# A graph layer's kernel: five edge groups gather normalised rows instead of weighted ones, and the weighted rows are made in the edge steps

## What is computed

```python
N_NODES, D, E = 6250, 512, 100000        # dst is sorted and dense at low numbers
xn = layernorm(x)
gnn = segment_sum(edge_weight[:, None] * xn[src], dst) @ Wg + bg
q, k = elu(xn @ Wq + bq) + 1, elu(xn @ Wk + bk) + 1   # 8 heads of 64
v = xn @ Wv + bv
mix = (q * z) @ (k^T v) @ Wp + bp        # linear attention, z = 1 / (q . sum of k)
x = x + gnn + mix
z = layernorm(x)
# FFN of 512 -> 256 -> 512 whose weights are merged by a gate: mean over rows of
# relu(z @ gfc1^T) @ gfc2^T gives 8 factors; W1m = W1 + sum g_e tv_W1[e], likewise b1, W2, b2
h = relu(z @ W1m^T + b1m)
out = x + layernorm(z + h @ W2m^T + b2m) * lng + lnb
```

## Time and profile before

| | us |
|---|---|
| median of 3 timed executions | 1598.65 (1595.19 to 1599.21) |
| the profiled execution | 1604.54, span 1602.7 |
| PE busy | 1385.1 (86%) |
| DVE busy | 1015.7 (63%) |
| POOL busy | 843.4 (53%) |
| ACT busy | 648.3 (40%) |
| mean granted clock of PE | 0.946 |
| moved by DMA | 366.46 MB |

### The profile page before, as it was taken

The page is one execution under the profiler, slowest core; times in us unless marked ns, Lnnn a source line. Parts: engine busy times, 40 slices in busy tenths (PEclk is TensorE's granted clock), DMA queues, the critical chain, the costliest instruction groups (busy, mean ns, idle before and its releaser), DMA issues. The chain is left out here.

```text
span 1602.7 us, 24972 instructions
## 1 busy us (share of the span) xinstructions
PE 1385.1 (86%) x7963; PEld 605.9 (38%) x7963; DVE 1015.7 (63%) x2041; ACT 648.3 (40%) x1045; POOL 843.4 (53%) x882
## 2 busy tenths in 40 slices
PE   4988978898889888998898988998995998889893
PEld 2544423333333333333333433433342443633331
DVE  7978634344343434385666667877878675448997
ACT  4787722222222322033333323333333665256663
POOL 0001267777777777477777777777771000033432
PEclk9999989999999999699999999999997999899996
DMA  6989678888888888477777777777777879514432
GB/s 214 312 310 341 242 247 274 272 267 271 261 260 274 268 267 290 138 238 237 230 237 236 237 229 234 240 242 250 230 224 183 220 197 223 158 60 151 157 138 85
DMA packets 201553, 366.46 MB, mean 229 GB/s; under 512 B 77101, under 2 KB 82879, under 8 KB 201441
## 3 DMA queue, kind: packets, MB, share of 16 engines
q0 software_dynamic: 62720, 205.57, 41.9%
q1 hardware_dynamic: 138000, 158.43, 30.7%
q10 hardware_dynamic: 720, 1.06, 0.2%
HBM read 287.93 MB, written 65.38 MB: 220 GB/s over the span
## 5 line engine op out<-in xcount | busy, mean ns | idle before, releaser
L1165 POOL DMA_INDIRECT rows<-y_rows,idxT x516 | 492.4, 954 | 184.6 <-issue 165.7
L919 ACT ACTIVATE mb<-bank,ones,ncols 128x512 f32<-128x512 f32 x98 | 76.3, 779 | 445.8 <-PE bank L1964 445.8
L1519 DVE SCALAR_TENSOR_TENSOR acc<-bank,maskt,acc 128x512 f32 x196 | 138.0, 746 | 102.3 <-PE bank L2072 81.9
L2060 PE MATMUL bank<-rows,hots 128*32 128x512 f16 x1548 | 118.1, 412 | 55.5 <-DMA rows<-y_rows,idxT 47.2
L1964 PE MATMUL bank<-Wg,xtb 128*128 128x512 f16 x588 | 139.1, 388 | 16.1 <-DVE xtb L1453 8.9
L1964 PE MATMUL bank<-ztg,G 128*128 128x512 f16 (+1 forms) x624 | 130.7, 371 | 15.5 <-DMA ztg<-zhigh 14.1
L1964 PE MATMUL bank<-KVP,qT 128*128 128x512 f16 x588 | 143.9, 397 | 0.0
L1964 PE MATMUL bank<-Wk,xta 128*128 128x512 f16 x588 | 139.5, 388 | 0.0
L1964 PE MATMUL bank<-Wq,xta 128*128 128x512 f16 x588 | 139.2, 388 | 0.0
L1200 POOL TENSOR_TENSOR acc<-acc,lnbb 128x512 f32 (+1 forms) x49 | 66.0, 1349 | 116.4 <-ACT zq L1051 116.4
L2044 PE MATMUL bank<-xr,kh 128*128 128x512 f16 x392 | 123.7, 399 | 2.4 <-DVE kl L1546 2.4
(11 more groups left out here) (311 smaller groups left out, 2428.9 us busy)
## 6 DMA issues: line engine op xcount, KB each, us to landing
xta<-xt_rows SPq DMA_DIRECT2D x98, 256.0 KB
x_rows<-xhl SPq DMA_DIRECT2D x49, 256.0 KB, 3.8
xt_rows<-xtb SPq DMA_DIRECT2D x49, 256.0 KB, 3.9
y_rows<-yb SPq DMA_DIRECT2D x49, 256.0 KB, 3.6
xr<-x_rows SPq DMA_DIRECT2D x49, 256.0 KB
zt_rows<-ztg SPq DMA_DIRECT2D x49, 256.0 KB, 2.3
acc<-in_x SPq DMA_DIRECT2D x48, 256.0 KB, 4.2
xd<-zt_rows SPq DMA_DIRECT2D x12, 1024.0 KB, 5.4
```

Source lines behind the costliest of these rows:

```text
L919: nc.scalar.activation(mb[:, :], of[:, :], ACT.Relu, scale=ncols[:, col:col + 1], bias=ones[:, 0:1]).then_inc(f_min, 1)
L1165: pool.indirect_dma_start(out=row_slot(s, k).rearrange("p a d -> p (a d)"), out_offset=None, in_=y_rows, in_offset=bass.IndirectOffsetOnAx ...
L1519: nc.vector.scalar_tensor_tensor(out=flat(acc, tile + m), in0=edge_bank(n)[:, :], scalar=maskt[:, m, n:n + 1], in1=flat(acc, tile + m), op ...
L2060: ins = nc.tensor.matmul(edge_bank(n)[W * k:W * k + W, :], hots[:, r, p, :, hot_column(s, k)], row_slot(s, k)[:, q, :], start=s == FIRST[n ...
```

## The change

- The y product, its two evictions and the store of `y_rows` leave the head. They come into the edge steps as slots of their own, -5 to 35 (`y_slots`: six tiles in five slots), from `xta`, which SP loads back from `xt_rows`; the products use four banks.
- The first five groups (16, 8, 8, 8 and 4 steps: XSTEPS = 44 steps) gather from `x_rows`, so POOL's gathers begin when `x_rows` and `xt_rows` are stored. Their placed sums come out transposed (four f32 matmuls of 128 columns), ACT and DVE split them in two f16 halves (`agg_higher`, `agg_lower`), and PE multiplies them by the gnn weight (`weigh`, 12 matmuls); the addition comes three slots later.
- k tiles move to slots 36 to 100, six in eight slots (before: six in ten), the turn stage to 103, q tiles to 108 to 188, six in ten (before: six in thirteen).
- The ring of row slots starts with three steps and has a fourth from step 16 on (before: five up to step 74).
- In the head, `xtb` has four buffers instead of two. The gnn weight's maximum, scale and split move from ahead of the loop into it; the splits of Wk and Wq and the packing of the edges move into the edge steps.
- In the last stage hT's low half is made by POOL (`hidden_rest`) instead of DVE (all but the first quad); h32 now holds the scaled value.

```diff
-K_FIRST, K_NUM, K_DEN = -2, 10, 6
+XG = 5
+XSTEPS = sum(LONG[:XG])
+AGG = 2.0 ** -27
+PLACES_AT, WEIGHTS_AT = 16, (4, 8)
+Y_FIRST, Y_NUM, Y_DEN, Y_BANKS = -5, 5, 6, 4
+K_FIRST, K_NUM, K_DEN = 36, 8, 6
 TURN = K_FIRST + K_NUM * (T - 1) // K_DEN + 3
-Q_FIRST, Q_NUM, Q_DEN = TURN + 5, 13, 6
+Q_FIRST, Q_NUM, Q_DEN = TURN + 5, 10, 6
...
-    free, homes = list(range(RING + 2)), []
+    free, homes = list(range(RING)), []
     for s in range(NGR):
+        if s == PLACES_AT:
+            free.insert(0, RING)
...
+            def keep_y(t):
+                sp.wait_ge(y_low, t + 1)
+                sp.dma_start(row_tile(y_rows, t), yb[:, t % 2].rearrange("p a d -> p (a d)")
+                             ).then_inc(y_kept[t % 2], 16)
+
+            for t in range(T + 2):
+                if t < T:
+                    load_turned(t, t)
+                if t >= 2:
+                    keep_y(t - 2)
+            sp.wait_ge(low_made, 3)
             for t in range(T + 1):
                 if t < T:
-                    load_turned(t, t)
+                    load_turned(T + t, t)
                 if t >= 1:
                     load_rows(t - 1)
+                if 8 <= t < 15:
+                    pack_edges(t - 8)
...
-            act.dma_start(Wgraw[:, :, :], gnn_w.rearrange("(c p) n -> p c n", p=P)).then_inc(w_loaded[0], 16)
             act.wait_ge(consts_made, 1)
             nc.scalar.activation(root[:, :], epsc[:, :], ACT.Sqrt)
+            act.wait_ge(x_loaded[1], 16)
+            act.dma_start(Wgraw[:, :, :], gnn_w.rearrange("(c p) n -> p c n", p=P)).then_inc(w_loaded[0], 16)
...
+            def agg_higher(n):
+                act.wait_ge(agg_turned, n + 1)
+                at_least(act, placed, n)
+                nc.scalar.activation(aggT[:, 0].rearrange("p c m -> p (c m)"), edge_bank(n)[:, :], ACT.Copy, scale=AGG
+                                     ).then_inc(agg_high, 1)
...
             head_kept(pool)
-            pool.wait_ge(y_made, T)
             limit = pool.to_reg(T * P - 1)
 
             for s in range(NGR):
+                if s == XSTEPS:
+                    for b in range(2):
+                        pool.wait_ge(y_kept[b], 16 * ((T + 1 - b) // 2))
...
-                    pool.indirect_dma_start(out=row_slot(s, k).rearrange("p a d -> p (a d)"), out_offset=None, in_=y_rows,
+                    pool.indirect_dma_start(out=row_slot(s, k).rearrange("p a d -> p (a d)"), out_offset=None,
+                                            in_=x_rows if s < XSTEPS else y_rows,
...
+            def hidden_rest(g, j):
...
+                    nc.gpsimd.tensor_tensor(hT[:, par, 1, o, 0:n], h32[:, o, 0:n], hT[:, par, 0, o, 0:n], ALU.subtract
+                                            ).then_inc(low_made, 1)
...
-            weight_largest(0, Wgraw).then_inc(maxes_made, 1)
             statistics(head, 0, 0, Q4)
-            y_scale()
             scales(head, 0, 0, Q4)
-            weight_low(0, Wg16, Wgraw, low_made, 0, 1)
-            head_ticks(head_tick, T + 3)
-
+            head_ticks(head_tick, T + 2)
+
+            def y_lower(t):
+                dve.wait_ge(y_high, t + 1)
+                nc.vector.scalar_tensor_tensor(out=yb[:, t % 2, 1, :], in0=y_bank(t)[:, :], scalar=cols[:, 0:1],
+                                               in1=yb[:, t % 2, 0, :], op0=ALU.mult, op1=ALU.subtract).then_inc(y_low, 1)
...
-                if j % Q4 in (1, 2) and not (isinstance(quad, int) and quad + 1 >= NQ):
-                    hidden_low(quad + 1, (j // Q4 + 1) % 2, P if isinstance(quad, int) and quad + 1 == NQ - 1 else Q4 * P,
-                               [j % Q4 - 1])
...
-            head_ticks(head_tick, T + 2)
-
-            def k_product(t):
+                at = tile_at(g, j)
+                if at == SPREAD_AT + 1:
+                    spread_starts()
+                if at - 1 in TURN_AT:
+                    turn_edges(TURN_AT.index(at - 1))
+
+            head_ticks(head_tick, T + 1)
+
+            def y_product(t):
 
                 b = t % 2
                 pe.wait_ge(xt_in[b], 16 * (t // 2) + 16)
+                at_least(pe, y_low, t - Y_BANKS + 1)
+                accumulate(y_bank(t)[:, :], [(xta[:, b, p, c, :], Wg16[:, q, c, :]) for c in range(C) for p, q in PASSES]
+                           ).then_inc(y_made, 1)
...
                 pe.wait_ge(placing, n + 1)
+                if n < XG:
+                    for c in range(C):
+                        s = slice(c * P, (c + 1) * P)
+                        ins = nc.tensor.matmul(edge_bank(n)[:, s], part32[:, n % 2, s], plc[:, n % (3 * WG), :],
+                                               start=True, stop=True)
+                    ins.then_inc(agg_turned, 1)
+                    return
...
+            def weigh(s):
+
+                n = ending(s)
+                if n is None or n >= XG:
+                    return
+                pe.wait_ge(agg_low, n + 1)
+                accumulate(edge_bank(n)[:, :], [(aggT[:, p, c, :], Wg16[:, q, c, :]) for c in range(C) for p, q in PASSES]
+                           ).then_inc(placed, 1)
...
+                weigh(s - 3)
+                for t in y_slots(s):
+                    y_product(t)
```

More of the change, by code:

```diff
@@ L67 @@
 U_HOT = 4
[L68 removed]
+H_HIGH, H_LOW = 3 + 2 * C, 3 + 2 * C
 OUTSIDE = float(1 << 20)
@@ L467, in exists, with y_slots, y_bank @@
             return not isinstance(g, int) or 0 <= tile_at(g, j) < T
+        def y_slots(s):
+            return [t for t in range(T) if Y_FIRST + Y_NUM * t // Y_DEN == s]
+        def y_bank(t):
+            return bank[t % Y_BANKS]
         def k_slot(t):
@@ L487, in head_kept @@
         def head_kept(eng):
[L489 to L492, removed]
             for i in range(4):
+                eng.wait_ge(head.turned_kept[i], 16 * ((T + 3 - i) // 4))
                 eng.wait_ge(x_kept[i], 16 * ((T + 3 - i) // 4))
@@ L957, in kv_rows @@
                                          ).then_inc(kvp_out, 1)
-            act.wait_ge(y_low, T)
-            act.wait_ge(pool_set, 20)
-            for s in range(K_FIRST, SLOTS_END):
+            act.wait_ge(head.low, T)
+            act.wait_ge(pool_set, 22)
+            for s in range(Y_FIRST, SLOTS_END):
+                for t in y_slots(s - 1):
+                    y_higher(t)
+                if s == WEIGHTS_AT[0]:
+                    weight_high(1, Wk16, Wkraw)
+                if s == WEIGHTS_AT[1]:
+                    weight_high(2, Wq16, Wqraw)
+                n = ending(s - 2)
+                if n is not None and n < XG:
+                    agg_higher(n)
                 for slot_of, after, work in ((k_slot, 1, k_feature), (q_slot, 1, q_feature), (k_slot, 2, k_higher),
@@ L1670, in tile_at_group @@
                 return dve.value_load(tileof[0:1, n:n + 1], min_val=0, max_val=T - 2)
[L1672 to L1675 removed]
+            dve.wait_ge(pool_set, 22)
+            for s in range(Y_FIRST, SLOTS_END):
+                for t in y_slots(s - 1):
+                    y_lower(t)
+                for k, w16, raw in ((1, Wk16, Wkraw), (2, Wq16, Wqraw)):
+                    if WEIGHTS_AT[k - 1] < s <= WEIGHTS_AT[k - 1] + 2:
+                        weight_low(k, w16, raw, low_made, s - WEIGHTS_AT[k - 1] - 1, 2)
+                n = ending(s - 2)
+                if n is not None and n < XG:
+                    agg_lower(n)
+                if n is not None and n >= XG:
+                    add_group(n, tile_at_group(n))
+                n = ending(s - 5)
+                if n is not None and n < XG:
                     add_group(n, tile_at_group(n))
```

223 lines of the change are left out of this document (107 added, 116 removed).

## The result

The changed kernel takes 1669.0 us (1667.4 to 1671.7), the kernel before on the same chip 1596.9 (1594.1 to 1599.2): a ratio of 1.045, 95% interval 1.043 to 1.048, 72 us slower. The forecast was 1606, in a range to 1637: the sign was the likelier one, the size was not in the range. The profiled execution after has a span of 1665.5 us.

The account below looks back on a forecast made before the run. PE was to become the edge stretch's bound (1007 us against the gathers' 980): 52 us earlier at the start, 60 more behind it, edges 7 to 10 later, 2 back in the last stage, so +7: 1606 us, range 1577 to 1637.

Parts of the forecast that it names:

- Head: Head loop: takes 132 us (bounds 126 and 145), last normalisation at 143, first gather at 152 instead of 204.
- Start and y steps: Edge start to step 36: step 0 at 177, POOL waits 11 us, then sets 5.0 us a step; part 36 at 352.
- The rival of slow y steps: Y steps and last stage: late transfers and port limits give 1631; decided by a y step over 5.2 us; chance 0.24.
- y to k: Change from y to k products: first k product waits 6 us for evictions, store issue and load, starting at 361.
- The k steps: Steps 36 to 100: 350 us of PE work plus 16 of waits, 361 to 727; turn stage reached at 736.
- bare pairs: K steps: k products following another with no m product between wait for bank 5, 16 us in all (bounds 0 and 25).
- Turn stage: Between k and q steps: keeps its 41 us, PE-bound at half clock for much of it; q starts at 777.
- q steps: Steps 108 to 188: 418 us plus 5 for coupling with DVE, ending at 1200; tail 25 us against 22.
- PE becomes the bound: Edge stretch: PE's work comes to 1007 us against 980 for the gathers, so the earlier gathers' 52 us cannot be had in full.
- my sign for error: K steps: the prediction is wrong if PE idles over 5% there.
- Last stage: Half of hT's rounding moved to POOL takes 19 us off DVE, 17 lost to stretching: 2 us gain (bounds 10 gain, 12 loss).
- 1640 by gathers that start late: Edge steps: rival in which POOL is held and early gathers do nothing, about 1640; chance 0.04.

Follow-up runs that it names:

- kf first: Changed kernel with VectorE making kf first in each edge step, ahead of the k lower half, k sum and three one-hot operations: 1625.1 us.
- kh first: Changed kernel with ScalarE making kh of the k tile before ahead of relu and exp of the newest tile: 1621.5 us.
- middle spread: Changed kernel with kf first, k products in 12 of 17 steps, q products in 12 of 19: 1630.0 us.
- early loads: First two xta loads for k products issued ahead of the last y stores: middle spread 1630.0 to 1621.5 us; 2 of 3 with kh first 1595.4 to 1591.0.
- fastest arrangement of the whole change: Changed kernel with k and q products in 2 of 3 steps, kh first and early loads: 1591.0 us.
- dense spread: Kernel before with k products in 3 of 4 steps instead of 3 of 5, q products in 2 of 5, no y products in edge steps: 1703.6 us.
- 2 of 3: Changed kernel with k products in 2 of 3 steps instead of 3 of 4, q products in 2 of 3 instead of 3 of 5: 1606.1 us.

## Why the prediction was right or wrong

- **Head, right.** First gather at 155.2 (forecast 152), last normalised tile's turn at 150.3; DVE busy 113.8 us, as summed (113).
- **Start and y steps, right.** First part at 178.7 (177); POOL then stood still for 9.6 us (11). Part 36 began at 359.8 (352), at 5.0 us a step, a DMA share of 0.95 and 325 GB/s; PE waited 28.6 us for `xta` in 25 places, which the gathers' pace covers. The rival of slow y steps fell, its point was 5.2.
- **y to k, right in place.** 6.06 us of wait for `xta`, k at 366.8 (361), the first product at half clock. This wait wasn't needed: two loads moved in SP's queue took 4 to 9 us off.
- **The k steps, wrong: the price of the bare pairs.** The forecast had named the wait on `kf` at these places, but put it at 16 us with a bound of 25, and it measured 74: 51 of waits and 23 of half-clock matmuls. These 58 us are nearly all of the miss of 63; the other terms' errors cancel to within some us. Two things were left out. First, I took the bare chain of the earlier trace rows (product, relu, exp, kf: 2.3 us), read in a step in which an m product hid the rest, and didn't write out what stands ahead of `kf` and `kh` in each queue; kf first and kh first, which change nothing else, take 29 to 32 us off the waits and remove the slow matmuls (kh first all but the one behind the first pair). Second, I let an idle PE cost only its idle time. The trace of before had the nearer row, the only bare pair in it, at the start of the k products (PE's waits, 205 to 1216 us), and I had not used it:

```profile
PE bank L1964 <- DVE kf L1539: 3.8, 1, 3.8
```

The product behind that wait ran slow as well:

```profile
214.83 5.19 PE L1964 MATMUL bank<-Wk,xta 128*128 128x512 f16 x12
```

- **Turn stage, 9 us better:** 31.8 us instead of 41, for its clock was 0.93 where the earlier trace rows has 0.67. The change doesn't account for it. From the last m product to the first q product the kernel before takes 40.9 us, and before with the last stage's edit alone, whose edge steps are the same, 32.4 at a clock of 0.90. With kf first it is 40.8 at 0.67, with the middle spread and early loads 36.2 at 0.76, and in the ten other kernels 28.7 to 32.6 at 0.85 to 0.94. What sets the clock there stays open.
- **q steps, right:** 430.3 us from first to last product (423), 20.6 of it waits on `qhl`, and 27.6 to the end (25).
- **PE becomes the bound: right as a sum, and as a bound in the q steps only.** 994 us busy in the fastest arrangement of the whole change, for a forecast of 1007. In the kernel as changed it was not full in the k steps (380 of 433): its idle time set the pace there, and my sign for error, idle over 5%, has come.
- **Last stage, right in kind, at its bound:** 10 us of gain for my 2, within the bounds of 10 and -12. The step that failed is the charge of 0.65 us on DVE for each POOL instruction: cen and ob lengthened by 0.10 us a tile, which is 0.19 for each of the 26 POOL instructions. The Trainium skill ("SBUF — State Buffer", section "Who interferes with whom") has it that a DVE instruction with two SBUF inputs contends with a GpSimd instruction that reads SBUF, one with a single SBUF input does not, and that the order of issue decides which of the two is held up. That res, with one input in PSUM, stays at 0.742 us agrees with it. The forecast had taken one direction only from it; the trace says that here it is mostly POOL that is held up.
- **Chances.** Slower had 0.48. The rivals on that side were 1631 by late transfers and ports, which gained 10 us in place of losing 10, and 1640 by gathers that start late, where the first came at 155.2. No rival was made of the term with the least support, the price of a wait that the trace of before "doesn't show".

That leaves what the y products' move is worth: with orders and spread mended and the loads early it comes to 1591, with the last stage's edit in it; that edit without the move gives 1586. The gathers start 49 us earlier, and 44 of these are paid back: from the first gather to the end of the edges it takes 1055.8 us in place of 1012.2, with PE busy 991 us in place of 905. Beside that last kernel, whose edges end at 1204.6, the move loses some 6 us.

## What to carry to other kernels

When an edit brings two users of one buffer next to each other, write out the queue of each engine between them, in program order, and price the wait by the last of these instructions, not by the bare chain; then look in the trace for the one place where the new neighbours already meet. An operation whose input is long ready must not stand behind one that waits for the newest result: moving it, on an engine that was busy 39%, was worth 48 us. And measure an edit's parts alone, since a loss can hide a gain that is worth keeping.

## What the runs showed of the hardware

I had not expected that short idle times of PE cost twice. In the place shown above the granted clock was 0.83 from 509.90 to 513.60 us, while PE waited, 0.51 over the product behind it, and 1.00 from 519.40 on: the lower level lasted through the one product, and the part behind it took 0.88 us as ever.

The length of the wait alone doesn't decide. Behind the eight waits of 3.73 and 4.06 us in the changed kernel all products were slow (six of 5.2 to 5.3 us, two of 4.4, for 2.75). Behind waits of 2.67 us four of six ran at full clock there, and none of six in the kernel before with the dense spread (4.05 to 5.30). Ahead of the second k product there is a wait of 3.0 us in nine kernels: the product took 2.75 us in four of them and 4.0 to 5.3 in five. Behind waits of 1.6 to 1.9 us, with kf first, kh first or the middle spread, it was always 2.75. Yet with kh first, 2 of 3 and early loads the second k product took 5.32 us behind a wait of 1.25, which followed two others of 0.78 and 1.66 within the 7 us before. What separates these cases, the runs don't tell.
